# First norm of a graph network: the row one-hot as 17 comparisons on VectorE, all of the centring on GpSimd, the normalising on VectorE

## The reference, cut to what matters

```
h = relu(layernorm(x))                       # the stage that is changed here
x = x + segment_sum(mlp(concat(h[row], h[col])), row)
h = relu(layernorm(x))
x = x + gin(h)                               # segment sum, two products, batch norm
```

## Time and profile before

| | us |
|---|---|
| median of three runs (1983.5 to 1986.97) | 1985.07 |
| the profiled execution | 1981.82 |
| its span, first to last instruction | 1979.3 |
| the stage `prepare`, from its first transfer to the next stage's | 77.86 to 310.00 |

### The profile page before, as it was taken

How to read it: one execution, slowest core, us unless ns; L and a number is a source line. 1 busy time by engine, 2 the same in 40 slices (tenths; PEclk the granted TensorE clock), 3 DMA queues, 4 the chain that set the end, 5 groups by cost and what they waited for, 6 DMA issues and landing times. The chain is left out here.

```text
span 1979.3 us, 37799 instructions
## 1 busy us (share of the span) xinstructions
PE 1428.0 (72%) x10165; PEld 1067.5 (54%) x10165; DVE 1063.9 (54%) x3259; ACT 975.3 (49%) x2310; POOL 1071.2 (54%) x1151
## 2 busy tenths in 40 slices
PE   0033337999999999999999994666556556566566
PEld 0022225777777777777777784443434334334334
DVE  4899993555555555555555555443443433433344
ACT  0188885776777777677777763111111111111144
POOL 0388884454444445445444542776666666666600
PEclk9999999999999999999999997777777777777765
DMA  1255544444554554455455453222222222222259
GB/s 34 61 125 130 122 109 115 125 119 119 130 129 110 128 135 115 122 129 127 111 129 136 111 138 73 58 57 55 47 53 51 50 54 46 54 54 46 33 180 340
DMA packets 435913, 200.77 MB, mean 101 GB/s; under 512 B 382585, under 2 KB 408710, under 8 KB 435866
## 3 DMA queue, kind: packets, MB, share of 16 engines
q1 hardware_dynamic: 343384, 142.00, 27.7%
q0 software_dynamic: 28224, 32.57, 9.1%
q10 hardware_dynamic: 64258, 25.65, 4.5%
HBM read 131.49 MB, written 55.79 MB: 95 GB/s over the span
## 5 line engine op out<-in xcount | busy, mean ns | idle before, releaser
L821 POOL DMA_INDIRECT fast_gathered<-h_table,fast_gather_i x441 | 423.2, 960 | 471.8 <-PE bank L963 295.0
L1180 POOL DMA_INDIRECT fast_gathered<-h_neighbours_table,fast_index_i x441 | 425.8, 966 | 197.4 <-POOL fast_index_i L1176 104.9
L1080 ACT ACTIVATE fast_h<-bank,b_s 128x384 f32<-128x384 f32 (+1 forms) x490 | 299.7, 622 | 177.7 <-PE bank L990 140.4
L1241 PE MATMUL node_sums<-twice,fast_self_rows 128*64 128x128 f32 x784 | 139.0, 423 | 279.3 <-DMA fast_gathered<-h_neighbours_table,fast_index_i 275.2
L1241 PEld LDWEIGHTS node_sums<-twice,fast_self_rows 128*64 128x64 f32 x784 | 120.5, 222 | 317.5 <-issue 307.0
L1272 ACT ACTIVATE fast_z_in<-node_sums 128x512 f32<-128x512 f32 x49 | 29.3, 597 | 517.7 <-PE node_sums L1247 517.7
L1087 ACT ACTIVATE fast_h<-fast_h 128x384 f32<-128x384 f32 (+1 forms) x490 | 263.8, 558 | 0.0
L1226 DVE BATCH_NORM_STATS2 z_stats<-z_t (+1 forms) x48 | 33.3, 694 | 386.2 <-ACT z_t L1283 386.2
L999 PE MATMUL bank<-fast_h,w_s 128*128 128x384 f32 (+1 forms) x490 | 235.3, 562 | 2.8 <-ACT fast_h L1087 1.9
L1247 PE MATMUL node_sums<-fast_hot,fast_gathered 128*64 128x256 f32 (+1 forms) x980 | 217.4, 444 | 0.0
L1034 PE MATMUL node_sums<-fast_message,fast_hot 128*128 128x80 f32 x1568 | 200.9, 276 | 0.0
(11 more groups left out here) (234 smaller groups left out, 2578.9 us busy)
## 6 DMA issues: line engine op xcount, KB each, us to landing
fast_local<-local_rows SPq DMA_DIRECT2D x49, 576.0 KB, 5.5
h_neighbours_table<-fast_h_rows SPq DMA_DIRECT2D x49, 320.0 KB
fast_self_rows<-h_neighbours_table SPq DMA_DIRECT2D x49, 320.0 KB, 3.3
h_table<-prep_normed ACTq DMA_DIRECT2D x49, 256.0 KB, 2.7
fast_own_rows<-h_table SPq DMA_DIRECT2D x49, 256.0 KB
fast_own_cols<-h_cols SPq DMA_DIRECT2D x49, 256.0 KB
x_plus_h<-fast_total SPq DMA_DIRECT2D x49, 256.0 KB, 6.4
finish_resid<-x_plus_h SPq DMA_DIRECT2D x49, 256.0 KB, 4.0
```

The costliest lines, as they stand in the source:

```text
L821: pool.indirect_dma_start(gathered[slot][:, j * D:(j + 1) * D], None, h0_t, bass.IndirectOffsetOnAxis(ap=gather_i[q][:, n:n + 1], axis=0))\
L1080: A(to[at][:, 0:w], psum[:, 0:w], ACT.Exp, bias=b_s[:, :]).then_inc(done, 1)
L1180: pool.indirect_dma_start(gathered[q][:, c * MW:(c + 1) * MW], None, h1_t, bass.IndirectOffsetOnAxis(ap=index_i[q][:, c:c + 1], axis=0))\
L1241: nc.tensor.matmul(banks[6 + q % 2][h * D:(h + 1) * D, k * P:(k + 1) * P], self_rows[q][:, at:at + D], twice[:, :], start=(k == 0), stop=F ...
```

## The change

The row one-hot becomes 17 instructions, one for each edge column: the fixed row of 0 to 127 is compared with one number per partition. `centre` on GpSimd takes all 512 columns, and `centre_rest` is gone with its semaphore. The eight Relu activations of ScalarE are replaced by one VectorE instruction, max(centred, 0) times the broadcast `prep_rstd`. This normalising runs one step later (lag 4 on VectorE), and so do the turning, the store and the keeping of columns.

```
                         def centre(b, q, turn):
                             hold(pool, mean_done, b + 1, passed_pool)
                             wait_from(pool, normed_done, b - RING + 1, passed_pool)
-                            G.tensor_tensor(groups(centred[q][:, :], D)[:, 0:ON_POOL], groups(xin[q][:, :], D)[:, 0:ON_POOL],
-                                            mean[q][:, 0:ON_POOL].unsqueeze(2).to_broadcast([128, ON_POOL, D]),
+                            G.tensor_tensor(groups(centred[q][:, :], D), groups(xin[q][:, :], D),
+                                            mean[q][:, :].unsqueeze(2).to_broadcast([128, SUBS, D]),
                                             ALU.subtract).then_inc(centred_done, 1)
...
-                            V.tensor_tensor(groups(row_hot[q % 2][:, :], P),
-                                            f[:, :, 1:2].to_broadcast([128, RAW, P]),
-                                            iota_h[:, :].unsqueeze(1).to_broadcast([128, RAW, P]),
-                                            ALU.is_equal).then_inc(row_hot_ready, 1)
+                            for n in range(RAW):
+                                last = V.tensor_scalar(row_hot[q % 2][:, n * P:(n + 1) * P], iota_h[:, :],
+                                                       f[:, n, 1:2], None, ALU.is_equal)
+                            last.then_inc(row_hot_ready, 1)
...
-                        def centre_rest(b, q, turn):
-                            dve.wait_ge(mean_done, b + 1)
-                            wait_from(dve, normed_done, b - RING + 1)
-                            V.tensor_tensor(groups(centred[q][:, :], D)[:, ON_POOL:SUBS], groups(xin[q][:, :], D)[:, ON_POOL:SUBS],
-                                            mean[q][:, ON_POOL:SUBS].unsqueeze(2).to_broadcast([128, SUBS - ON_POOL, D]),
-                                            ALU.subtract).then_inc(rest_centred, 1)
...
+                        def normalise(b, q, turn):
+                            wait_from(dve, stored[q], 16 * turn)
+                            wait_from(dve, cols_turned, b - RING + 1)
+                            dve.wait_ge(rstd_done, b + 1)
+                            V.scalar_tensor_tensor(groups(normed[q][:, :], D), groups(centred[q][:, :], D), 0.0,
+                                                   rstd[q][:, :].unsqueeze(2).to_broadcast([128, SUBS, D]),
+                                                   ALU.max, ALU.mult).then_inc(normed_done, 1)
...
-                        rounds(dve, [(0, sum_columns), (3, variance), (1, centre_rest), (0, row_hots)], BLOCKS)
+                        rounds(dve, [(0, sum_columns), (3, variance), (4, normalise), (0, row_hots)], BLOCKS)
...
-                        rounds(pe, [(0, pack), (4, turn_cols)], BLOCKS)
+                        rounds(pe, [(0, pack), (5, turn_cols)], BLOCKS)
...
-                            for k in range(SUBS):
-                                at = slice(k * D, (k + 1) * D)
-                                last = A(normed[q][:, at], centred[q][:, at], ACT.Relu, scale=rstd[q][:, k:k + 1])
...
-                        rounds(act, [(0, scale_mean), (3, log_variance), (1, square), (1, move), (3, invert), (3, normalise), (4, store),
-                                     (5, keep_cols)],
+                        rounds(act, [(0, scale_mean), (3, log_variance), (1, square), (1, move), (3, invert), (5, store),
+                                     (6, keep_cols)],
                                BLOCKS)
```

More of the change, by code:

```diff
@@ L492, in prepare @@
                      "normed_done", "unpacked"))
-                cols_turned, cols_kept, rest_centred = s("cols_turned"), s("cols_kept"), s("rest_centred")
-                ON_POOL = 6
+                cols_turned, cols_kept = s("cols_turned"), s("cols_kept")
                 from_sub_ready, local_turned, local_moved, local_stored = (
@@ L511, in load_x @@
                             wait_from(sp, centred_done, b - RING + 1, passed_sp)
-                            wait_from(sp, rest_centred, b - RING + 1, passed_sp)
                             if is_last(b):
@@ L649, in square @@
                             act.wait_ge(centred_done, b + 1)
-                            act.wait_ge(rest_centred, b + 1)
                             wait_from(act, var_done, b - RING + 1)
@@ L662, in invert @@
                             A(rstd[q][:, :], log_var[q][:, :], ACT.Exp, scale=-0.5).then_inc(rstd_done, 1)
[L664 to L667, removed]
-                            for k in range(SUBS):
-                                at = slice(k * D, (k + 1) * D)
-                                last = A(normed[q][:, at], centred[q][:, at], ACT.Relu, scale=rstd[q][:, k:k + 1])
-                            last.then_inc(normed_done, 1)
                         def move(b, q, turn):
```

## The result

The changed kernel takes 2076.07 us in the median (2075.69 to 2078.01, four runs) against 1984.28 for the kernel before on the same chip (1983.41 to 1986.97, four runs): 1.0462 times as long, interval 1.0444 to 1.048. That is 91.8 us slower; 2088 was forecast, with 2010 to 2123 as the range.

What follows compares the result with a forecast made beforehand. VectorE's queue was taken to bound the `prepare` stage. Per step 0.43 + 0.03 + 1.77 = 2.23, times 49 is 109.3, less 1.8 and 4.1: +103.4 us, giving 2088 us, range 2010 to 2123.

Steps and rivals of the forecast that it cites:

- What bounds the stage, and what the step is made of: In `prepare`, VectorE's queue sets the stage: five instructions, 4.33 us a step, 49 steps 212 of 232 us.
- The comparison's pitch: 17 row one-hot comparisons at 0.163 us each, 2.77 against 2.34 a step: +0.43, bounds -0.13 and +0.98.
- The normalising: One VectorE instruction with pitch 0.60 us where `centre_rest` stood with 0.57: +0.03 a step.
- GpSimd gets in between two comparisons: In the train, `spread_fields` enters after the first comparison, `centre` right behind; later comparisons wait for both.
- The hold: VectorE's wait for GpSimd in the train: 0.83 for `spread_fields` plus 1.08 less 0.14 for `centre`, +1.77 us a step.
- Rival A: GpSimd is locked out until the train ends, then delays the normalising by 0.70: +51, 2036 us; chance 0.11.
- Rival B: 16-bit comparisons and GpSimd do not shut each other out: 2002 us, or 2029 with the f32 pitch; chance 0.17.
- C: Faster: comparison columns free (pitch 0.13), GpSimd out of the way, -0.10 a step, 1974 us; chance 0.05.
- D: Worse: f32 comparison pitch and full hold, 2.78 a step, 2115 us, or 2123; above 2123 has chance 0.05.
- Start and end: Fewer normalisings ahead of the last one-hot, -1.8 us; 14.1 instead of 18.2 us behind it, -4.1.
- ScalarE's saving bought nothing: ScalarE loses eight activations, 2.0 us a step, but was not the bound, so no gain in the middle.
- TensorE's wait: TensorE waits 81.5 / 29 = 2.8 us a step for `prep_spread`, so the later pack is covered.

Runs made afterwards that it cites:

- The two halves measured alone: Kernel before with only the 17 comparisons: 2056.37 us (1.0363); changed kernel with the single row one-hot comparison put back: 2006.64 us (1.0111).
- the second half: Centring and normalising alone: the changed kernel with the single row one-hot comparison put back; 2006.64 us, 1.0111 of the kernel before.
- the last experiment: Kernel before with row one-hot laid out edge innermost, row numbers copied first, and VectorE normalising one of eight groups, ScalarE seven: 0.9809 of the kernel before.

## Why the prediction was right

*What bounds the stage, and what the step is made of.* Right. VectorE is busy 50.00 of 50.00 after the change too, and the difference lies in the stage.

*The comparison's pitch.* 0.163 was taken between 0.13 and 0.195, 0.1625 came out; 17 of them cost 2.76, the forecast was 2.77. The reason given for halving the column part, that half of the bytes move, was a choice, and no run tests it by itself. The Trainium skill (VectorE: DVE Perf Modes, "The perf-mode tier table") has four columns a cycle for this kind; by that rule, the trace agrees: over the fixed 0.13 taken from the f32 trains, 0.0325 us are left for 128 columns.

*The normalising.* 0.60 in place of 0.57: right (204.43 to 205.03).

*GpSimd gets in between two comparisons.* Right, and shown from three sides: the stretches vanish when nearly all of GpSimd's work does (step 4.82), when the compared row comes from PSUM (longest 0.415), and the one beside `prep_spread` when it runs under the reductions (step 5.57). The hold begins one comparison later than forecast, at the third of the train. Rival A, GpSimd locked out until the train has ended, is refuted by `prep_spread` at 0.97 us inside the train. Rival B, no exclusion by 16-bit comparisons, is refuted by the comparisons of 1.08. C fails with them: its pitch of 0.143 was not reached, and the hold is not zero. D's pitch was not there. One reading under this was thinner than it said: the earlier trace rows has GpSimd beside both reductions, so it shows 0.67 us "with" and not "without". The changed kernel gives the other half: 0.67 for the variance at 203.84, with GpSimd idle.

*The size of the hold* is the one term that was off: 1.77 forecast, 1.55 measured (0.71 beside `prep_spread`, taken as 0.83, and 0.84 beside `centre`, taken as 0.94). I had carried 0.83 over whole from the place where GpSimd waited behind one long instruction. In a train each run of GpSimd costs VectorE 0.20 to 0.26 us less than it lasts (0.71 of 0.97, 0.84 of 1.04, 0.62 of 0.83), and the runs of 0.24 and 0.28 cost next to nothing. I read that as the comparison in front still running while GpSimd starts; no run shows the reason by itself. 49 x 0.22 = 10.8 us; 103.4 less 10.8 is 92.6, and 91.8 was measured.

*Start and end.* 14.1 us were forecast behind the last one-hot; from 386.84 (382.45 + 4.39) to the next stage it took 14.3:

```profile
382.45 4.39 DVE L568 TENSOR_SCALAR prep_row_hot<-iota_h,prep_raw 128x128 f16<-128x128 f16 x17
...
391.52 0.76 DVE L595 SCALAR_TENSOR_TENSOR prep_src_f<-prep_packed 128x441 f32<-128x441 f32 x1
...
401.12 0.40 SPq L756 DMA_DIRECT2D fast_own_rows<-h_table  x1
```

*ScalarE's saving bought nothing*, as forecast: about 2 us a step came off an engine that was not the bound.

*The two halves measured alone* cost 1.0363 and 1.0111 of the time before, together 4.7% against 4.6% for the whole. That they add up is luck, not a sign that they are independent. In the run with the single comparison the extra 0.61 us a step are a normalising stretched from 0.67 to 1.26 (pitch 1.18, in place of `centre_rest`'s 0.57). In the changed kernel nothing stretches the normalising; there the second half costs 0.40 because `centre_rest` alone would take only 0.20 of VectorE's queue, and 0.22 because the wider `centre` holds a comparison for longer.

*TensorE's wait.* 81.5 / 29 = 2.8 us is the mean of 29 waits, not of all steps: in the 42 steps from 100 to 280 us the other 13 waits, 35.6 us, were for the row one-hot. The mean of all is 2.8 too, and nothing rested on the difference.

## What to carry to other kernels

When VectorE and GpSimd work at the same time, look at where GpSimd's instructions fall, not only at how long each engine is busy. One long VectorE instruction with two SBUF inputs keeps GpSimd off for its whole length and lets it run under reductions, which it does not disturb; split into short ones it gives GpSimd the turn in the middle, and VectorE waits. An instruction that shows 3 us for 459 columns on GpSimd may be 1 us of work behind somebody else's lock, so read its end against the other engine's end before costing it. And an engine that shows no gap need not be the bound: compare its step with the sum of its instructions when nothing stretches them (3.60 and 3.34 in the kernel with the edge innermost).

## What the runs showed of the hardware that I had not expected

A change of turn is close to free: with GpSimd's instructions at 0.24 and 0.28 us the train of 17 took 17 free pitches in about half of the steps and 0.04 us more in the mean, while at 0.97 and 1.04 us they cost 0.71 and 0.84.

Even a VectorE copy of 17 columns is shut out until GpSimd's run has ended: 0.83 us (201.39 to 202.22, `centre` to 202.18), where the same copy in the last experiment, with nothing beside it, takes 0.17:

```profile
204.17 0.17 DVE L585 COPY prep_rows<-prep_raw 128x17 f16<-128x17 f16 x1
```

The Trainium skill (SBUF — State Buffer, "Who interferes with whom") names copies among those that can take the shared pair; by that rule, the trace agrees.

A 16-bit comparison of two tensors goes through nearly twice as many columns per us when the broadcast is over the outer dimension and not the innermost: 2,304 columns in 1.34 us, against 2,176 in 2.41. That layout made a kernel 1.7 to 1.9% faster than the one before.
